# Experts on units of 128 rooms instead of tiles of 256

## What is computed

```python
# first layer, cut: the recurrence and its experts
gate = sigmoid(h @ Wh.T + z_t @ Wz.T + b)
h    = tanh(h * (1.0 - alpha) + gate * z_t)          # 256 steps
_, idx = top_k(softmax(xt @ gate_w + gate_b), 2)     # xt: all h, 4096 rows of 256
mask   = one_hot(idx, 8).sum(axis=1) > 0
h1     = relu(einsum('th,ehf->etf', xt, w1) + b1)    # 256 -> 1024
out_e  = einsum('etf,efh->eth', h1, w2) + b2         # 1024 -> 256
x      = x + einsum('eth,te->th', out_e, mask)
```

## Time and profile before

| | |
|---|---|
| median of 3 runs | 1268.68 us (1264.85 to 1269.13) |
| the profiled execution | 1267.8 us |
| its span, first to last instruction | 1264.8 us |
| TensorE busy | 1123.6 us, 89% |
| VectorE busy | 892.9 us, 71% |
| ScalarE busy | 583.3 us, 46% |
| GpSimd busy | 250.9 us, 20% |

### The profile page before, as it was taken

How to read it: one execution, slowest core, us unless ns; L and a number is a source line. 1 busy time by engine, 2 the same in 40 slices (tenths; PEclk the granted TensorE clock), 3 DMA queues, 4 the chain that set the end, 5 groups by cost and what they waited for, 6 DMA issues and landing times.

```text
span 1264.8 us, 32645 instructions
## 1 busy us (share of the span) xinstructions
PE 1123.6 (89%) x10732; PEld 864.7 (68%) x10733; DVE 892.9 (71%) x3002; ACT 583.3 (46%) x1782; POOL 250.9 (20%) x289
## 2 busy tenths in 40 slices
PE   6777777787768999999999999889999999987895
PEld 4665666565557999998899999746766666763263
DVE  5677677676775587965555555468898889987875
ACT  3555555555553444444444444362445533434373
POOL 1002112112114675343333333300000000001001
PEclk9999999999999999999999999989999999998998
DMA  6222333233233475343333333243000000000035
GB/s 174 76 72 89 90 97 97 82 93 109 71 91 106 102 166 133 91 70 59 58 53 60 62 62 62 36 132 134 2 1 1 0 1 0 1 1 1 1 51 83
DMA packets 57527, 84.36 MB, mean 67 GB/s; under 512 B 7361, under 2 KB 47170, under 8 KB 57410
## 3 DMA queue, kind: packets, MB, share of 16 engines
q1 hardware_dynamic: 41186, 57.94, 16.1%
q0 software_dynamic: 16224, 24.96, 10.9%
HBM read 51.36 MB, written 35.70 MB: 69 GB/s over the span
## 4 chain that ended last, share of the span: by engine, by line
PE 75%; ACT 9%; DVE 9%; issue 3%; DMA 1%; SPq 1%; POOL 0%; DVEq 0%; ACTq 0%; POOLq 0%
PE ps L570 23%; PE ps L1105 16%; PE ps L1117 16%; PE ps L1660 7%; DVE ps L1589 5%; PE ps L1665 4%; ACT work L1516 4%; ACT ps L1511 3%; DVE imax L986 2%; PE ps L924 2%; PE ps L1630 1%; PE ps L1086 1%; ACT W L955 1%; PE ps L1638 1%; PE ps L911 1%
## 5 line engine op out<-in xcount | busy, mean ns | idle before, releaser
L1141 ACT ACTIVATE lane<-ps,b_now 128x256 f32<-128x256 f32 x312 | 147.4, 474 | 240.1 <-PE ps L1105 216.4
L1105 PE MATMUL ps<-lane,W 128*128 128x256 f16 x1872 | 213.3, 274 | 2.2 <-ACT lane L1129 1.3
L1117 PE MATMUL ps<-W,lane 128*128 x1872 | 210.7, 273 | 0.0
L1105 PEld LDWEIGHTS ps<-lane,W 128*128 x1872 | 184.0, 98 | 25.1 <-issue 2.8
L1117 PEld LDWEIGHTS ps<-W,lane 128*128 128x128 f16 x1872 | 181.5, 98 | 20.4
L1660 PE MATMUL ps<-work 128*128 128x16 f16 x2048 | 99.1, 177 | 89.5 <-ACT work L1516 88.8
L1660 PEld LDWEIGHTS ps<-work 128*128 128x128 f16 x2048 | 76.3, 107 | 141.3 <-ACT work L1516 139.9
L1284 POOL DMA_INDIRECT results<-lane,dest x78 | 123.8, 1588 | 231.3 <-DVE lane L1198 195.8
L570 PE MATMUL ps<-W,work 128*128 128x512 f16 x768 | 168.7, 382 | 0.0
L1210 DVE TENSOR_TENSOR lane<-lane 128x256 f16<-128x256 f32 x312 | 133.4, 427 | 10.8
L570 PEld LDWEIGHTS ps<-W,work 128*128 128x128 f16 x768 | 74.9, 98 | 90.1 <-issue 2.2
(11 more groups left out here) (214 smaller groups left out, 1533.7 us busy)
## 6 DMA issues: line engine op xcount, KB each, us to landing
lane<-rows SPq DMA_DIRECT2D x39, 257.0 KB
stage<-in_w1T SPq DMA_DIRECT2D x16, 512.0 KB, 3.7
stage<-in_w2T SPq DMA_DIRECT2D x16, 512.0 KB, 4.0
b_now<-in_b SPq DMA_DIRECT2D x39, 128.0 KB
work<-in_zT SPq DMA_DIRECT2D x32, 128.0 KB, 2.2
results<-in_xn SPq DMA_DIRECT2D x32, 128.0 KB
W<-results SPq DMA_DIRECT2D x8, 512.0 KB, 3.8
out<-W SPq DMA_DIRECT2D x8, 512.0 KB, 4.9
```

The costliest lines, as they stand in the source:

```text
L1105: last = pe.matmul(ps[:, f % 4, 0:ST], of_e(W1[:, bass.ds(e, 1), a, k, f * P:(f + 1) * P]), xT[:, p, b, k], start=(i == 0 and k == 0), sto ...
L1117: last = pe.matmul(ps[:, 4 + q, 0:D], hid[:, a, f, q * P:(q + 1) * P], of_e(W2[:, bass.ds(e, 1), b, f]), start=(i == 0 and f == 0), stop=( ...
L1141: act.activation(v4[:, f % 4], ps[:, f % 4, 0:ST], ACT.Relu, bias=b1_now[:, p, f:f + 1], scale=A_SCALE / W_SCALE).then_inc(l1_v, 1)
```

## The change

A unit of work is now 128 rooms (ST = 128), so SQ is 1 and SLOT_TILES = (8192 + 8 x 127) // 128 = 71. Each unit has the same chunks and products as a tile had: in the first layer 48 matmuls of 128 columns, in the second 24 of 256 columns, and four transposes. ScalarE writes a whole unit's values to a buffer of eight chunks (v8), and VectorE splits two chunks in one instruction (PAIR = 2), with one semaphore step for the pair; in the second layer TensorE waits once a pair. The result of a unit goes to its own PSUM bank by parity, so TensorE waits for the result of the unit before the last. There is one result scatter a unit. GpSimd now fetches the destinations of the next unit before it scatters the last results. The numbers of units written out (JOBS = 29), of the first unit with a job (FIRST_JOB = 10) and of the units in the early table (EARLY = 32) are about doubled, and the other work is spread over them anew, one thing a unit. Some buffers move in SBUF.

```diff
-ST = 256
+ST = 128
 SQ = ST // P
 PAIRS = 2 * N
 SLOT_TILES = (PAIRS + E * (ST - 1)) // ST
-JOBS = 15
-FIRST_JOB = 5
-EARLY = 16
+JOBS = 29
+FIRST_JOB = 10
+EARLY = 32
+PAIR = 2
...
+        obuf = part(2 * SQ * D).rearrange("p (b q d) -> p b q d", b=2, q=SQ)
+        hid_v = part(4 * FC * ST, F16)
+        hid = hid_v[:, 0:2 * FC * ST].rearrange("p (s f n) -> p s f n", s=2, f=FC)
+        v_flat = hid_v[:, 2 * FC * ST:].bitcast(F32)
+        v8 = v_flat.rearrange("p (f n) -> p f n", f=FC)
         v32 = v_flat.rearrange("p (b n) -> p b n", b=2)
-        obuf = part(2 * SQ * D).rearrange("p (b q d) -> p b q d", b=2, q=SQ)
+        hq = [a.bitcast(BF16).rearrange("p (f n) -> p f n", f=FC) for a in (hid_v, xs_flat)]
+        w1qT = part(DC * F, BF16).rearrange("p (k f) -> p k f", k=DC)
+        w2qT = part(FC * D, BF16).rearrange("p (f d) -> p f d", f=FC)
...
-                if not is_tile(n, 0):
-                    pe.wait_ge(out_ready, n)
+                if not (is_tile(n, 0) or is_tile(n, 1)):
+                    pe.wait_ge(out_ready, n - 1)
                 for f in range(FC):
-                    pe.wait_ge(l1_hid, FC * n + f + 1)
+                    if f % PAIR == 0:
+                        pe.wait_ge(l1_hid, FC // PAIR * n + f // PAIR + 1)
                     for i, (a, b) in enumerate(((0, 0), (1, 0), (0, 1))):
                         for q in range(SQ):
-                            last = pe.matmul(ps[:, 4 + q, 0:D], hid[:, a, f, q * P:(q + 1) * P],
+                            last = pe.matmul(ps[:, 4 + SQ * p + q, 0:D], hid[:, a, f, q * P:(q + 1) * P],
                                              of_e(W2[:, bass.ds(e, 1), b, f]), start=(i == 0 and f == 0),
                                              stop=(i == 2 and f == FC - 1))
                 last.then_inc(l2_psum, 1)
-                if is_tile(n, 0):
+                if is_tile(n, 1):
...
-                act.activation(xT[:, p].rearrange("p s k n -> p (s k n)"), psh(6), ACT.Copy).then_inc(xT_ready, 1)
+                act.activation(xT[:, p].rearrange("p s k n -> p (s k n)"), psh(6)[:, 0:2 * DC * ST], ACT.Copy).then_inc(xT_ready, 1)
...
-                    if not (is_tile(n, 0) and f < 4):
-                        act.wait_ge(l1_hid, FC * n + f - 3)
-
-                    act.activation(v4[:, f % 4], ps[:, f % 4, 0:ST], ACT.Relu, bias=b1_now[:, p, f:f + 1],
+                    if f % PAIR == 0 and not is_tile(n, 0):
+                        act.wait_ge(l1_hid, FC // PAIR * (n - 1) + f // PAIR + 1)
+
+                    act.activation(v8[:, f], ps[:, f % 4, 0:ST], ACT.Relu, bias=b1_now[:, p, f:f + 1],
...
+        LAST_OPS = (range(0, 8), range(8, 13), range(13, 21), range(21, 29), range(29, ROUTE_OPS + LATE_OPS))
...
-                dve.scalar_tensor_tensor(obuf[:, p], ps[:, 4:4 + SQ, 0:D], 1.0 / (W_SCALE * A_SCALE), b2_,
+                dve.scalar_tensor_tensor(obuf[:, p], ps[:, 4 + SQ * p:4 + SQ * p + SQ, 0:D], 1.0 / (W_SCALE * A_SCALE), b2_,
                                          ALU.mult, ALU.add).then_inc(out_ready, 1)
 
             def tile(n, m, p):
                 if not is_tile(n, 0):
                     results(n - 1, m - 1 + p, 1 - p)
-                for f in range(FC):
-                    dve.wait_ge(l1_v, FC * n + f + 1)
-                    if f == 0 and not is_tile(n, 0):
+                for h in range(FC // PAIR):
+                    pair = slice(PAIR * h, PAIR * h + PAIR)
+                    dve.wait_ge(l1_v, FC * n + PAIR * h + PAIR)
+                    if h == 0 and not is_tile(n, 0):
                         dve.wait_ge(l2_psum, n)
-                    dve.tensor_copy(hid[:, 0, f], v4[:, f % 4]).then_inc(split0, 1)
-                    dve.wait_ge(split0, FC * n + f + 1)
-                    dve.tensor_tensor(hid[:, 1, f], v4[:, f % 4], hid[:, 0, f], ALU.subtract).then_inc(l1_hid, 1)
-                    if is_tile(n, 0):
-                        for k in range(2 * f, min(2 * f + 2, 13)):
-                            route_op(dve, BATCHES - 1, k)
-                    if is_tile(n, 1):
-                        for k in range(13 + 2 * f, min(15 + 2 * f, ROUTE_OPS)):
-                            route_op(dve, BATCHES - 1, k)
-                        if f >= 3:
-                            for k in range(2 * f - 6, 2 * f - 4):
-                                late_table_op(dve, k)
-                    if is_tile(n, 2):
-                        for k in range(10 + 2 * f, min(12 + 2 * f, LATE_OPS)):
-                            late_table_op(dve, k)
+                    dve.tensor_copy(hid[:, 0, pair], v8[:, pair]).then_inc(split0, 1)
+                    dve.wait_ge(split0, FC // PAIR * n + h + 1)
+                    dve.tensor_tensor(hid[:, 1, pair], v8[:, pair], hid[:, 0, pair], ALU.subtract).then_inc(l1_hid, 1)
+                    if isinstance(n, int) and n < len(LAST_OPS):
+                        ops = LAST_OPS[n]
+                        for k in range(ops.start + 2 * h, min(ops.start + 2 * h + 2, ops.stop)):
+                            if k < ROUTE_OPS:
+                                route_op(dve, BATCHES - 1, k)
+                            else:
+                                late_table_op(dve, k - ROUTE_OPS)
                 if isinstance(n, int):
                     at = n - FIRST_JOB
-                    if 0 <= at < 4:
-                        for c in range(2 * at, min(2 * at + 2, 7)):
-                            split_piece(dve, c)
-                    if 4 <= at < 8:
-                        scale_piece(dve, at - 4)
-                    if 5 <= at < 9:
-                        quantise_piece(dve, at - 5)
-                    if at == 3:
+                    if 0 <= at < 7:
+                        split_piece(dve, at)
+                    if at in (8, 10, 12, 14):
+                        scale_piece(dve, at // 2 - 4)
+                    if at in (9, 11, 13, 15):
+                        quantise_piece(dve, at // 2 - 4)
+                    if at == 7:
...
-        LAST_ROWS = {1: range(0, 2), 2: range(2, 5), 3: range(5, 8)}
-        LAST_PADS = {4: range(0, 3), 5: range(3, 6), 6: range(6, 9), 7: range(9, 12), 8: range(12, 14), 9: range(14, 16)}
+        FIRST_ROW, FIRST_PAD = 3, 11
...
+                if not is_tile(n, SLOT_TILES - 1):
+                    destination(n + 1, m + p, 1 - p)
                 if not is_tile(n, 0):
                     store_results(n - 1, 1 - p)
-                if not is_tile(n, SLOT_TILES - 1):
-                    destination(n + 1, m + p, 1 - p)
-                if n == 1:
+                if n == FIRST_ROW:
                     rows_to_scatter(pool, BATCHES - 1)
-                for k in LAST_ROWS.get(n, ()):
+                k = n - FIRST_ROW
+                if 0 <= k < 2 * RING:
                     scatter_row(pool, BATCHES - 1, k // RING, k % RING)
-                if n == 4:
+                if n == FIRST_PAD:
                     pool.wait_ge(table_ready, 2)
-                for k in LAST_PADS.get(n, ()):
-                    scatter_pad(pool, k // 2, k % 2)
+                k = n - FIRST_PAD
+                if 0 <= k < SQ * E:
+                    scatter_pad(pool, k // SQ, k % SQ)
 
             for n in range(SLOT_TILES):
                 tile(n, n // 2, n % 2)
...
                 if is_tile(n, JOBS - 1):
...
-                    for c in range(2 * at + 2, min(2 * at + 4, 8)) if at < 4 else range(at + 4, min(at + 5, len(pieces))):
-                        load_piece(c)
+                    if at < 7:
+                        load_piece(at + 2)
+                    if at in (9, 11):
+                        load_piece(at // 2 + 5)
```

More of the change, by code:

```diff
@@ L171, in build_program @@
         hrow_at = 9216 - HELD * RING * ROW // 2
-        zero_at = hrow_at - ROW
+        zero_at = hrow_at - ROW // 2
         assert zero_at >= 1024 + 1024 + 1024 + 512 + 256 + 256 + 512 + 256
-        pad_at = 9216 - ROW
+        pad_at = 9216 - ROW // 2
         pad_rows = work[:, pad_at:pad_at + SQ * (D + 1)].rearrange("p (q n) -> p q n", q=SQ)
-        zero_rows = work[:, zero_at:zero_at + ROW].rearrange("p (q n) -> p q n", q=SQ)
+        zero_rows = work[:, zero_at:hrow_at].rearrange("p (q n) -> p q n", q=SQ)
         hrow = work[:, hrow_at:].bitcast(F16).rearrange("p (t n) -> p t n", t=HELD * RING)
@@ L180, in build_program @@
         stage = sb("stage", [P, 2, 1024], F32)
-        lane = sb("lane", [P, 6144 + 2 * SQ], F32)
+        lane = sb("lane", [P, 5120 + 2 * ST + SQ * ROW], F32)
         part = carve(lane[:])
@@ L189, in build_program @@
         xT = part(2 * 2 * DC * ST, F16).rearrange("p (b s k n) -> p b s k n", b=2, s=2, k=DC)
-        w1qT = xg_flat[:, 0:DC * F].bitcast(BF16).rearrange("p (k f) -> p k f", k=DC)
-        w2qT = xT.rearrange("p b s k n -> p (b s k n)").bitcast(BF16).rearrange("p (f d) -> p f d", f=FC)
-        hid = part(2 * FC * ST, F16).rearrange("p (s f n) -> p s f n", s=2, f=FC)
-        hq = [a.bitcast(BF16).rearrange("p (f n) -> p f n", f=FC)
```

(19 more changed lines are left out.)

## The result

The changed kernel takes 1398.33 us (median of four runs, 1396.97 to 1399.57), the kernel before 1267.72 beside it on the same chip (1264.85 to 1269.13). The ratio is 1.1033, with a 95% interval of 1.101 to 1.1057: 10% slower. The forecast was 1400.

A forecast was written before the change was run, and what follows sets the result against it. TensorE's sequencer, through address calculations, was to bind the changed kernel: 31 x 7.3 + 40 x 8.4 = 562 us against 429.5, +133; 1267.8 + 133 - 2 - 1 + 1 = 1399, given as 1400 us, range 1350 to 1455.

The forecast's parts named there:

- the main step: TensorE's sequencer in the expert stage: 48 address calculations a unit set the period, 7.3 us unrolled, 8.4 us looped.
- The signs: Expert stage: 32 and 16 calculations, 125 to 145 ns steps, falling TensorE share, periods 7.3 and 8.4, VectorE and ScalarE mostly idle.
- The rival of 80 ns: TensorE in the expert stage: weight load and matmul pairs take 80 ns, 6.8 us a unit, 1317 us; chance 4%.
- Address calculations don't bind: Expert stage: calculations hidden behind matmuls or fewer generated, 5.51 us a unit, 1232 us; chance 6%.
- The clock falls: TensorE in the expert stage drops to the 1.2 GHz level, 10.5 us a unit, 1580 us; chance 8%.
- The scatter chain: Result scatters of the expert stage, each waiting for the one before: 5.4 us, under the 7.3 us unit.
- Ends: Outside the unit periods: -2 for the last unit, -1 for the first transposes and copy, +1 for wider table operations.
- the first: End of the expert stage: one last scatter instead of two, -1.9 us, and a result half as wide, -0.2 us.
- The other two: First transposes and their copy halved, -1 us; wider table operations between calculations of the recurrence, below 1 us more.

The follow-up runs named there:

- An experiment that took them away: Changed kernel with the second layer alone at constant addresses (expert 0), the first layer's 32 calculations kept: 1336.85 us, ratio 1.0535.
- more calculations: Changed kernel with the first layer's second product on a slice shifted by 64 columns, 14 more address calculations a unit: 1523.19 us, ratio 1.2003.
- the two with the early load: Changed kernel, all unrolled, next number loaded before the unit's last wait: 1351.41 us with calculated addresses, 1274.52 with the second layer's constant.
- one slice: Changed kernel with registers kept but one weight slice for all matmuls of a layer, 2 calculations a unit instead of 48: 1242.81 us, ratio 0.9834.

## Why the prediction was right

**The time.** 1400 against 1398.33. The stage was put at 562 us and took 563.2. The mechanism is as foreseen; that the numbers agree to 2 us is in part luck. At the measured periods 31 x 7.28 + 40 x 8.31 is 558. The loop's 8.4 us a unit was put 4 us too high in sum, and the 5 us that the stage's first unit lost were not in the forecast.

**Calculations, the main step.** The prediction's 32 and 16 a unit are what the changed kernel issues, and their step in the first layer is 128 ns where 132 had been read at the stage's start. Adding 14 of them costs 126 to 129 ns each, taking nearly all away gives 1243, and the same edit in the kernel before gives nothing. 7.3 and 8.4 us a unit were foreseen, 7.28 (7.22 over a whole unrolled stage) and 8.31 came. Inside the unit at 410.7 the second layer's calculations lie from 414.8 to the load at 417.2, 2.4 us where 2.1 was summed, with a step of 153 ns and not 133; the first layer and the handover were somewhat shorter than put.

**The signs.** The counts, the first layer's step, the periods and the clock came as named. Three signs did not. TensorE's share hardly fell (88% after 89%), because the flights of its matmuls hide the gaps, so this sign can't tell. VectorE idles more than half of the time in the loop only; in the unrolled part it is busy for 68%, with its other jobs, and yet doesn't bind, as its pairs show. And the second layer's step lies above the 145 ns that were named.

**Where the step was too simple.** The sum treated the second layer's calculations as 0.133 us each on the path. They are only the longer of two things that run at the same time: the calculations of three pairs, and the time until VectorE's last pair is ready. The prediction had both numbers (1.9 and 1.2 us) and said that the difference would be lost if the cover went; it did not say that the reverse bounds what taking the calculations away can give. The total wasn't hurt, since in the changed kernel the calculations are the longer. An experiment that took them away was forecast 78 us wrong. Likewise matmuls and calculations are no clean "larger of the two": where the waits keep the sequencer beside the engine, a layer bound by the one and a layer bound by the other add.

**Matmuls and weight loads.** 55.6 ns a pair was read from 16 transposes, and a run with constant addresses has 61 ns with its waits and 2.75 us for 48 (57 ns) with the first layer alone constant. The rival of 80 ns is out, and with it the Trainium skill's figure ("TensorE: Matmul & The Clock Gate", "Back-to-back issue gap", some 81 ns for a pair at 128 columns) for this kernel.

**The rivals.** "Address calculations don't bind": out; its 1232 us is, nearly, what the kernel takes when they are gone (1237). "The clock falls": granted 1.00 in both stretches of the stage; from 382.27 to 397.11, its first unit with the stall of the last section, the mean was 0.64. It did fall, to 0.69 in the mean, in the kernel with branches, where TensorE paused for 8.6 to 14.7 us between units; the pauses of 0.3 to 0.8 us of the changed kernel were no such thing.

**VectorE, ScalarE, scatter.** Pairs gain nothing here that the time shows (ratio 1.1043 without them, 1.1033 with them). ScalarE takes 368 ns for 128 columns, below its bound of 474, and VectorE's cast 306, not 290. The scatter chain was put at 5.4 us, under 7.3 and so hidden; the run with constant addresses shows it at 5.58. Its parts were put otherwise: 3.79 to land, 0.3 between issues and 1.3 for another scatter behind it, where 4.5 to 5.1 and 0.8 are read, with no other scatter in those rows.

**Ends.** -2 together: the span grew by 2.0 less than the stage. Of the parts, the first is right: from the last matmul to the landing of the last scatter 813.5 to 820.15 became 945.48 to 950.07, 6.6 us and then 4.6. The other two were put at -1 and +1. Ahead of the stage 1.7 us were saved (384.01 to 382.27), and the stages behind took 1.8 more, which the prediction had not named and no run explains; here too the sum is better than its terms.

## What to carry to other kernels

Work that an engine's sequencer does for each tile, such as addresses worked out from a register, doesn't shrink with the tile: before halving a tile, count those instructions in the lines of the loop, multiply by their step where nothing holds them, and compare with the matmul time of the smaller tile. Here that was 48 calculations, 7.3 us with the load, against 5.5 us of matmuls. A share of busy matmuls can't show this bound, since gaps shorter than a matmul's flight are counted busy; the rate in the chain of waits can. When a run of fixed addresses shows what there is to win, ask what the replacement puts on the same sequencer: here a choice among eight copies put 12.2 us on each unit (17.8 against 5.6) to save 1.7 (7.3 against 5.6).

## What the runs showed of the hardware that was not expected

A branch of TensorE's sequencer took 65 ns at the least and 2.9 us in the median (up to 6.9 us at the loop's end) in a program whose copies of a unit are chosen by branches, with 5 MB more of instructions fetched; in the changed kernel the rolled loop's branch took 208 ns in the median.

The load of a number from SBUF to a register takes TensorE's sequencer 0.7 to 0.8 us to the first calculation that uses it (495.0 to 495.7, 417.2 to 418.0); moved ahead of a wait, about 0.5 us of it was hidden where the sequencer stood at that wait, and nothing where it didn't.

In the first unit of the stage ScalarE stood for 3.98 us between two chunks (the row at 385.99 above), in the changed kernel. The traces of six further runs have such a pause of 2.5 to 4.0 us: more calculations, each layer alone at constant addresses, the two with the early load, and the branches. Those of four don't, and have their first 48 matmuls in one row of 4.4 to 5.3 us: both layers at constant addresses, one slice, no pairs, and all units unrolled. These four ran on one chip, the six on two others, so the edit need not be what decides it. The changed kernel's stage holds 5 us above its periods, about the size of the pause. The profile names no releaser, and the cause is open.
